# The maxima's store and loads of the first stage, moved from the sync queue to the scalar engine's queue

## The reference, cut to what matters

```
# stage 0: 16 heads of width 8, a bias that depends on the distance of two tokens
proj = layernorm(x) @ w_in.T;  k, v, q = split(proj)
logits = q @ k.T / sqrt(8) + bias[head, i - j]
attn = softmax(logits);  x = x + layernorm(attn @ v)
# stage 1: the same sizes with other weights and no bias, then a projection,
# then experts: each token goes to one of 8 by the argmax of its gate
```

## Time and profile before

| what | value |
|---|---|
| median of 3 runs | 907.78 us (903.33 to 908.55) |
| the profiled execution, its own time | 911.31 us |
| its span, first to last instruction | 909.3 us |
| granted TensorE clock over the span | 0.944 |
| stage 0, loop of units 0 to 31 | from 55.66 us of the span, 12.25 us for a unit with nothing beside it |

### The profile page before, as it was taken

The page is one execution under the profiler, slowest core; times in us unless marked ns, Lnnn a source line. Parts: engine busy times, 40 slices in busy tenths (PEclk is TensorE's granted clock), DMA queues, the critical chain, the costliest instruction groups (busy, mean ns, idle before and its releaser), DMA issues.

```text
span 909.3 us, 23148 instructions
## 1 busy us (share of the span) xinstructions
PE 800.9 (88%) x9157; PEld 298.6 (33%) x9157; DVE 752.6 (83%) x1196; ACT 635.8 (70%) x1266; POOL 242.9 (27%) x548
## 2 busy tenths in 40 slices
PE   5179999989999999999999999998999999954950
PEld 2013334333333333343332223322232322234950
DVE  5389978988999998889999998898999999236734
ACT  6037777767776777777778989998989999921311
POOL 4110413200000315232300543342001401004773
PEclk9559999999999999999999999999999999976985
DMA  3565444545555445356313333332221121001313
GB/s 96 175 192 176 148 136 156 185 153 175 170 171 150 161 163 172 111 173 190 96 60 110 102 115 101 103 90 74 85 71 55 60 84 49 30 17 49 51 50 101
DMA packets 69472, 104.72 MB, mean 115 GB/s; under 512 B 15845, under 2 KB 45861, under 8 KB 69365
## 3 DMA queue, kind: packets, MB, share of 16 engines
q1 hardware_dynamic: 62805, 68.31, 25.3%
q10 hardware_dynamic: 5088, 31.92, 9.7%
q0 software_dynamic: 1472, 3.02, 1.6%
HBM read 84.19 MB, written 18.87 MB: 113 GB/s over the span
## 4 chain that ended last, share of the span: by engine, by line
PE 69%; DVE 9%; DMA 7%; SPq 4%; ACT 4%; issue 3%; POOL 3%; POOLq 0%; DVEq 0%
PE bank L1288 22%; PE bank L1307 20%; PE bank L1314 11%; PE bank L1268 7%; ACT prob_mem L901 4%; DVE unit_max L1003 4%; DMA maxima_rows<-max_rows 3%; PE bank L1472 2%; PE bank L1481 2%; DVE stats L946 1%; PE bank L1352 1%; DMA k_parts<-prob_mem 1%; PE bank L1234 1%; POOL moe_out L797 1%; PE bank L1241 1%
## 5 line engine op out<-in xcount | busy, mean ns | idle before, releaser
L901 ACT ACTIVATE prob_mem<-bank 128x512 f32<-128x512 f32 x1024 | 556.6, 596 | 143.8 <-PE bank L1314 119.1
L1268 PE MATMUL bank<-k_rows,q_rows 56*128 56x512 bf16 x1024 | 329.2, 394 | 24.3 <-DMA k_rows<-k_parts 14.7
L1307 PE MATMUL bank<-q_rows,k_rows 59*128 59x512 bf16 x1024 | 335.8, 387 | 10.0 <-DMA q_rows<-maxima_rows 6.0
L999 DVE CUSTOM_DVE_ANT_1 no_use<-bank,w_moe 128x1024 bf16<-128x1024 f32 x256 | 305.7, 1219 | 34.6 <-PE bank L1268 31.5
L1288 PE MATMUL bank<-prob_mem,v_ring 128*32 128x256 f32 x4096 | 321.1, 387 | 7.6 <-issue 6.5
L1003 DVE TENSOR_REDUCE unit_max<-bank 128x1 f32<-128x1024 f32 x256 | 297.5, 1216 | 17.0 <-PE bank L1268 15.2
L1307 PEld LDWEIGHTS bank<-q_rows,k_rows 59*128 59x128 bf16 x1024 | 81.8, 93 | 247.6 <-ACT prob_mem L901 116.2
L702 POOL CAST max_parts<-unit_max 128x8 bf16<-128x8 f32 x64 | 12.2, 191 | 559.5 <-DVE unit_max L999 317.1
L1288 PEld LDWEIGHTS bank<-prob_mem,v_ring 128*32 128x32 f32 x4096 | 102.7, 109 | 153.7 <-ACT prob_mem L901 62.2
L1314 PE MATMUL bank<-skew_mem,pick 96*32 96x512 bf16 x1664 | 138.4, 390 | 0.0
L1268 PEld LDWEIGHTS bank<-k_rows,q_rows 56*128 56x128 bf16 x1024 | 77.9, 93 | 34.9 <-issue 16.0
(11 more groups left out here) (177 smaller groups left out, 516.1 us busy)
## 6 DMA issues: line engine op xcount, KB each, us to landing
w_moe<-bias_rows ACTq DMA_DIRECT2D x31, 960.0 KB, 5.6
q_rows<-q_parts SPq DMA_DIRECT2D x252, 48.0 KB
k_rows<-k_parts SPq DMA_DIRECT2D x126, 96.0 KB
skew_mem<-bias_parts SPq DMA_DIRECT2D x32, 378.0 KB, 3.9
unit_sums<-o_ring SPq DMA_DIRECT2D x63, 128.0 KB, 2.5
w_moe<-in_L_ffn_w_dram SPq DMA_DIRECT2D x16, 256.0 KB, 2.9
q_parts<-prob_mem SPq DMA_DIRECT2D x8, 384.0 KB, 3.1
k_parts<-prob_mem SPq DMA_DIRECT2D x24, 128.0 KB, 2.8
```

Source lines behind the costliest of these rows:

```text
L901: nc.scalar.activation(prob[:, kb, half * N:(half + 1) * N], b_bank(("exp", exp_no(n, kb, half))), ACT.Exp).then_inc(exp_done, 1)
L999: nc.vector.tensor_tensor_reduce(out=no_use[:, qb % 2, :].rearrange("p (k c) -> p k c", k=QB), in0=scores.rearrange("p (k c) -> p k c", k= ...
L1268: return nc.tensor.matmul(sa_slot(QB * m + qb)[:, f, :], q_rows[rows, m % SLOTS, qb * P:(qb + 1) * P], k_rows[rows, m % SLOTS, f * N:(f + ...
L1307: return nc.tensor.matmul(b_bank(("exp", exp_no(n, kb, f))), k_rows[rows, n % SLOTS, kb * P:(kb + 1) * P], q_rows[rows, n % SLOTS, f * N:( ...
```

## The change

In stage 0 the store and the two loads of the maxima are issued by ACT. The store comes straight behind ACT's own copy at kb = 2 and waits for this copy's semaphore. The two loads come behind the exponentials of kb = 4 and wait for the store's landing. SP's list loses them for units 1 to 31; unit 0's and those of stage 1 stay with SP.

```
+        def store_maxima(queue, n):
+            queue.dma_start(maxima_dram[n % 2], max_rows[:, n % 2, :]).then_inc(mrow_stored, 16)
+
+        def load_maxima(queue, n):
+            slot = n % 2
+            queue.wait_ge(mrow_stored, 16 * (n + 1))
+            maxima = maxima_dram[slot].rearrange("(p q) c -> p (q c)", p=3)
+            for f in range(2):
+                queue.dma_start(q_rows[f * HP + KR:f * HP + KR + 3, n % SLOTS, f * N:(f + 1) * N],
+                                maxima[:, f * N:(f + 1) * N]).then_inc(mrow_loaded[slot], 16)
...
             def maxima_of(n):
-                (the store, the wait and the two loads, by sp)
                 sp.wait_ge(max_copied, n + 1)
+                store_maxima(sp, n)
+                load_maxima(sp, n)
...
-                if n + 1 < NU:
+                if U <= n + 1 < NU:
                     maxima_of(n + 1)
...
                     if kb == MAX_AT and n + 1 < NU:
                         maxima_out(n + 1, max_t(n + 1))
+                        if n + 1 < U:
+                            act.wait_ge(max_copied, n + 2)
+                            store_maxima(act, n + 1)
+                    if kb == MAX_AT + 2 and n + 1 < U:
+                        load_maxima(act, n + 1)
```

More of the change, by code:

```diff
@@ L497, in maxima_of @@
             def maxima_of(n):
-                slot = n % 2
                 sp.wait_ge(max_copied, n + 1)
[L501 to L506, removed]
+                store_maxima(sp, n)
+                load_maxima(sp, n)
             def store_sums(n):
```

## The result

| kernel | median | ratio to the kernel before, 95% interval |
|---|---|---|
| before | 905.52 us (6 runs, 900.23 to 908.55) | |
| changed | 917.69 us (6 runs, 909.24 to 921.16) | 1.0115 (1.0081 to 1.0148) |

The change makes the kernel slower, by 1.15% or about 10.4 us by the ratio (the two medians lie 12.2 us apart). Forecast were 905.5 us in a range of 900 to 917. The first rival's 917 us is about what came, and its mechanism too in the main: the wait for the store's landing moved to ACT.

A forecast was written before the change was run, and what follows sets the result against it. TensorE was taken to set the pace in stage 0. From the median of 907.78 us, 4.7 us gained and 2.5 us lost, -2.2 us in sum, gave 905.5 us, in a range of 900 to 917.

The forecast's parts named there:

- The first rival: Stage 0: landings stay slow and the wait moves to ACT, 12.5 us lost, 917 us in all; chance 0.11.
- What bounds the kernel: Stage 0: TensorE sets the pace, busy for 88% of the span, with the chain on it for 69%.
- the issue's cover on ACT: Behind ACT's copy: the store's issue of 0.33 us is hidden in 0.70 us of idle time before the next exponential.
- The gain, 4.7 us: TensorE's waits for the maxima at 203 and 450 us, units 11 and 30, both go: 3.58 and 1.15 us.
- The room, 2.98 us: On ACT, from the store's issue: time the landing may take before the first exponential of kb = 5 is delayed.
- no slack behind it: Behind ACT's wait: a wait longer than 2.98 us stops TensorE for the whole excess.
- The landing's cost, 2.5 us: ACT's wait for the maxima's store in stage 0: two units lose 1.25 us each; bounds 0 and 12.5 us.
- 14 gaps of before: Store-to-loads gaps in the earlier profile: 14 of 31 over 2.98 us, 54.2 us in sum, 12.5 us over it.
- SP's backlog: Transfers on q1, with 102.9% of the engines' time from 76 to 77 us, said to hold back the store.
- The moved rows, costed at nothing: SP's ten loads of rows for unit n + 4, issued at about 233.5 and not after 237: no cost.
- the second rival: Store behind the 960 KB table on ACT's queue, slowed by rows: 0.7 us lost per unit, 925 us; chance 0.14.

The follow-up runs named there:

- The second profile: The kernel before, unchanged, profiled once more: 907.44 us in the profiled execution, its 32 stage-0 periods 416.39 us.

## Why the prediction was wrong, point by point

- **What bounds the kernel, and the issue's cover on ACT**: right. TensorE sets the pace, the store's issue is hidden behind 0.70 us of idle time. (One reading was too wide: in the earlier trace rows not every engine was at work, GpSimd has 0.00; TensorE was busy for the whole stretch.)
- **The gain, 4.7 us**: there between these two profiles, but 3.58 of it was one unit of one execution that lay 6 us over the later median of the kernel. The second profile has 1.36 us at unit 30 and none at unit 11. I had written that this execution lay 3.5 us over the median and yet took its rarest wait as the rule.
- **The room, 2.98 us, and no slack behind it**: right. 1.44 us of excess cost 1.33, and a block less of room cost 1.7 us per unit.
- **The landing's cost, 2.5 us: this is the step that failed.** It measured 13.1 us in one profile and 10.4 in the other. The forecast had the upper bound of 12.5 us from 14 gaps of before, and took two units at 1.25 each in their place; instead ten units lost over 0.5 us. It chose the lower end on two grounds. The first, that the store on its own queue passes SP's backlog, is refuted by unit 18: q1 at 98 to 112%, q10 next to nothing. The second, that SP would be on time and the skewed table ahead of the big one, came true in every unit that lost over 0.6 us but 18, where SP waited for the sums' landing in its list, and it did not help: units 9, 10, 23, 28 and 29 had their skewed table 4.2 us ahead of the copy and lost 6.3 us together. To be on time does not make the landing fast.
- **The moved rows, costed at nothing**: wrong. TensorE did not wait for rows, but they stand ahead of the store now. With the rows put behind the landing 4 to 7 us of the loss go in the profiles and 7.7 by the timed ratios, and undisturbed landings are shorter: ACT, 2.6 us behind the store, no longer waits for them. I had a part of it, 0.6 us per unit, in the second rival only.
- **The rivals**: the first, with 0.11, gave the size and most of the mechanism. Part of the agreement in size is luck: its sum holds the gain of 4.7 us, most of which was one execution's, and no term for the moved rows. The second's ingredient, rows in front of the store, was at work in part.
- **The two rules named in the forecast**: the rule of the Trainium skill that gave the first rival's sum (DMA: Bandwidth & Descriptors, Issuing engines are not separate DMA queues: all issuers' transfers run on the same 16 engines, and a second issuer saves only issue time) is what the runs bore out: with the store on either queue the loss in units 2 to 29 is about the same, 5.8 and 5.0 us, once the rows are behind it. The Trainium skill's other rule there (Queues, rings and completion order), that each engine takes turns between the queues that it has work for, is not seen at work in unit 18 over two microseconds; whether the store's packets were ready by then the trace does not tell. In unit 29 both queues moved packets in the same microsecond.

## What to carry to other kernels

A wait for a landing belongs on an engine that nobody follows closely. ACT may issue the store that its own copy feeds, since TensorE leaves it idle there for 0.70 us anyway; the wait and the loads behind it belong here to SP, and moving a transfer to another queue does not take it out of the traffic. When a wait leaves a list, look at what moves up into its place: here the rows came in front of the very transfer that was to be quicker. And a gain that hangs on one wait in one profile needs a second profile first.

## What was not expected of the hardware

- A small transfer on ACT's queue, which had nothing else to do, moved no packet for two microseconds (285.5 to 287.5 us) while SP's queue used 100% of the engines' time; with either table small, in those two profiles, no exponential waited for it.
- The same 6 KB store landed in 1.27 us at the least and in 5.58 at the most in the kernel before, and 5.50 in the changed one. Rows issued ahead of it are a part of that, and so are the two bias tables; what part the stores of parts have is open, since no run took them away.
